# A state-space layer with a routed feed-forward, fp32, on one core: side jobs dealt out anew over the slots of the scan

## The reference

```python
x = x + _layernorm(attn(_layernorm(x)))
x = x + _layernorm(ffn(_layernorm(x)))

# attn, on resid = _layernorm(x):
resid_norm = resid * rsqrt(mean(resid * resid) + EPS) * norm_w
skip, x_in = resid_norm @ W_skip, resid_norm @ W_in            # 512 -> 1024
x = silu(conv(x_in) + conv_b)                                  # 4 taps, depthwise
delta = softplus(x @ W_delta_1 @ W_delta_2 + b_delta_2)
Bm, Cm = x @ W_B, x @ W_C                                      # 16 states
# scan over rows, for each of 1024 channels and 16 states:
h = h * exp(delta * A) + (delta * x) * B
y = sum(h * C over states)
out = resid + ((y + x * W_D) * silu(skip)) @ W_out

# ffn, on flat rows: softmax over 64 experts, top 8
out = flat * sum(topk_w) + topk_w @ expert_bias[topk_idx]
```

## Time and profile before

| what | value |
|---|---|
| median of 3 runs | 2427.64 us (2422.99 to 2432.9) |
| the profiled execution | 2433.15 us, span 2431.3 us |
| TensorE busy | 1988.2 us (82%) |
| GpSimd busy | 1918.7 us (79%) |
| VectorE busy | 1771.9 us (73%) |
| ScalarE busy | 1756.3 us (72%) |
| DMA | 425.91 MB, 175 GB/s on the mean |
| granted TensorE clock, mean | 0.941 |
| first scan starts, last scan ends | 150.24 us, 2294.67 us |

### The profile page before, as it was taken

The page is one execution under the profiler, slowest core; times in us unless marked ns, Lnnn a source line. Parts: engine busy times, 40 slices in busy tenths (PEclk is TensorE's granted clock), DMA queues, the critical chain, the costliest instruction groups (busy, mean ns, idle before and its releaser), DMA issues. The chain is left out here.

```text
span 2431.3 us, 35499 instructions
## 1 busy us (share of the span) xinstructions
PE 1988.2 (82%) x11589; PEld 1577.2 (65%) x11589; DVE 1771.9 (73%) x3121; ACT 1756.3 (72%) x3492; POOL 1918.7 (79%) x1192
## 2 busy tenths in 40 slices
PE   3757777888888898889889898888888888888884
PEld 3546666767586776758677676767667676757552
DVE  3347776879687887869787787968778696887732
ACT  1367877787777778687777868777786877877631
POOL 0158988898888889888888978888797978999812
PEclk9778998999999999999999999999999999999996
DMA  4355646555565646556475646656475545646320
GB/s 129 104 178 165 196 160 225 183 196 190 170 211 166 219 148 221 185 174 213 128 250 170 208 154 198 208 178 204 131 245 176 190 165 174 205 156 195 122 100 18
DMA packets 239025, 425.91 MB, mean 175 GB/s; under 512 B 18878, under 2 KB 135162, under 8 KB 238842
## 3 DMA queue, kind: packets, MB, share of 16 engines
q1 hardware_dynamic: 238842, 423.65, 53.3%
HBM read 347.57 MB, written 76.02 MB: 174 GB/s over the span
## 5 line engine op out<-in xcount | busy, mean ns | idle before, releaser
L597 POOL TENSOR_TENSOR hc<-h,c_all 128x1024 f32<-128x1024 f32 x512 | 1207.7, 2367 | 252.1 <-DVE h L965 246.0
L965 DVE TENSOR_TENSOR_SCAN h<-operand,carry,bank 128x512 f32<-128x512 f32 x480 | 591.5, 1269 | 210.4 <-ACT operand L690 127.7
L1156 PE MATMUL bank<-ident,u_t 128*128 128x128 f32 x2560 | 426.4, 292 | 296.6 <-DVE h L965 288.5
L1161 PE MATMUL y_sum<-ident,hc 128*128 128x128 f32 x4096 | 622.1, 284 | 6.0 <-POOL hc L597 5.3
L1156 PEld LDWEIGHTS bank<-ident,u_t 128*128 128x128 f32 x2560 | 301.7, 147 | 462.6 <-issue 241.6
L709 ACT ACTIVATE u_t<-dx_t,b_t 128x256 f32<-128x256 f32 x1280 | 576.4, 502 | 0.0
L1161 PEld LDWEIGHTS y_sum<-ident,hc 128*128 128x128 f32 x4096 | 509.3, 148 | 56.4 <-issue 38.1
L581 POOL TENSOR_TENSOR operand<-dx_q,b_all 128x1024 f32<-128x1024 f32 x192 | 454.1, 2365 | 20.5 <-DMA dx_q<-dx_dram 20.4
L690 ACT ACTIVATE operand<-delta_q,neg_a 128x512 f32<-128x512 f32 x640 | 433.0, 714 | 0.3
L965 DVE TENSOR_TENSOR_SCAN h<-bank,carry,operand 128x512 f32<-128x512 f32 x288 | 358.1, 1272 | 90.7 <-ACT bank L690 77.8
L690 ACT ACTIVATE bank<-delta_q,neg_a 128x512 f32<-128x512 f32 x384 | 263.0, 685 | 135.2 <-DVE h L965 133.6
(11 more groups left out here) (125 smaller groups left out, 2147.0 us busy)
## 6 DMA issues: line engine op xcount, KB each, us to landing
c_all<-bc_dram SPq DMA_DIRECT2D x256, 512.0 KB, 4.1
b_all<-bc_dram SPq DMA_DIRECT2D x192, 256.0 KB, 5.3
win<-in_L_attn_W_in SPq DMA_DIRECT2D x64, 512.0 KB, 4.6
wskip<-in_L_attn_W_skip SPq DMA_DIRECT2D x64, 512.0 KB, 3.8
xd_dram<-hv SPq DMA_DIRECT2D x64, 256.0 KB, 5.9
delta_dram<-delta SPq DMA_DIRECT2D x32, 512.0 KB, 5.4
dx_dram<-dx SPq DMA_DIRECT2D x32, 512.0 KB, 6.3
delta_q<-delta_dram SPq DMA_DIRECT2D x32, 512.0 KB, 5.4
```

The lines of the kernel that those rows point to most:

```text
L597: nc.gpsimd.tensor_tensor(hc[:, number % 3], h[:, number % 3], c_all[:, j % 2, s % 2:s % 2 + 1].to_broadcast([P, 2, SPAN]), ALU.mult).then ...
L965: nc.vector.tensor_tensor_scan(h[:, number % 3, q], first, second, start, ALU.mult, ALU.add).then_inc(scan_done.sem, 1)
L1156: last = transpose(bank[:, q, b * P:(b + 1) * P], u_t[:, j % 2, b, q * P:(q + 1) * P], ident[:])
L1161: return matmul(to, lhsT=of, rhs=ident[:], is_transpose=True, start=start, stop=stop, skip_group_check=True)
```

## The change

**Steps may be crossed.** The loop is now over `step` and `slot`, and `at(step, slot)` gives each side job's own slot number, which may lie before 0 or beyond 31, so that a job begins in the step before or ends in the one after. There is one more pass of the loop, for what hangs over.

**Where the jobs stand now:** `norm` 1 to 28 (moments 5, factors 7 to 9, scaling 12, transposes 23 and 24). `prep`: W_in of a pair in slots 3p-2 and 3p-1, first tap 3p, convolution 3p and 3p+1 (one tile each), tanh and x both 3p+3; W_delta_1 10 to 13, W_B and W_C 13 and 14, softplus 20 and 22, dx 21 and 23. `mix`: W_skip 3p+14, tanh, `gate` and `ys` all 3p+16, W_out 26 to 29 (two terms a slot) and 31 to 38, `z` 30 and 43. `route`: 13 to 47, that is up to slot 15 of the next step (top 8 in 34, `o` in 38 and 40, its scaling in 44, the last sum in 45). `take_y` in 18 and 2.

**TensorE's slot has two places for side work**, one after each half of the transposes (`side_work(step, slot, late)`); in slots 1 and 17 the last state of a quarter is added ahead of the transposes.

**Arithmetic that goes or comes.** `regate` goes: `prep`'s `rnt` is stored to `rnt_dram` and loaded again as `rnt_gate` (job `gate`). x D is no longer computed by ScalarE: x itself is stored, and `y_sum` starts with a product with a diagonal matrix `diag_d` (16 passes a quarter where it was 8 transposes). `xn` of chunk 0 and two pieces of W_in are loaded first. `o` has its own tile, `wt` shares that of `low`, `kept` has 6 entries. The four shared PSUM banks are called `mixed`, `routed` and `pair_banks`.

```diff
+        def at(step, slot):
+            return [(t, slot + (step - t) * SLOTS) for t in (step - 1, step, step + 1) if 0 <= t < len(jobs)]
...
             @block.sync
             def _(sp):
+                sp.dma_start(xn[:], x_rows[0:T, :].rearrange("(b p) d -> p b d", p=P)).then_inc(x_loaded.sem, 16)
                 for to, of in small_loads:
                     sp.dma_start(to, of).then_inc(router_in, 16)
+                for p in range(2):
+                    sp.dma_start(win[:, p], w_in_tiles[:, :, p * QE:(p + 1) * QE]).then_inc(win_loaded[p].sem, 16)
...
-                        if s == 1:
-                            take_y(t - 1, 1)
-                        if s == 17:
-                            take_y(t, 0)
+                        if slot == 2:
+                            take_y(step - 1, 1)
+                        if slot == 18:
+                            take_y(step, 0)
...
-                                if s == 3 * p + 5:
+                                    if s == 3 * p + 3:
                                         if v := due(act, conv_done, t, 2 * p + 2):
...
-                                if s == 3 * p + 4:
-                                    banks = pair_bank(p)[:].rearrange("p (e t) -> p e t", e=2)
+                                    if s in (3 * p, 3 * p + 1):
+                                        e = s - 3 * p
+                                        et = 2 * p + e
+                                        row, halo = hv[:, p % 2, e], edge[:, et]
...
+                                        link(weighed(row[:, 0:tail], got[:, 0:tail], tail, bias_over(tail) if fresh else halo))
+                                        for k in range(TAPS - 1):
+                                            reach = TAPS - 1 - k
+                                            part = halo[:, 0:reach]
+                                            done = weighed(part, got[:, T - reach:], k, part if k else bias_over(reach))
...
+                                            last = weighed(row[:, reach:], got[:, 0:T - reach], k, row[:, reach:])
+                                            if k < TAPS - 2:
+                                                link(last)
...
-                            for q in range(2):
-                                last = add_turned(y_sum[:, b, q * P:(q + 1) * P], xd_q[:, q, b * P:(b + 1) * P],
-                                                  b % 2 == 0 and q == 0, False)
+                            for q in range(2):
+                                last = matmul(y_sum[:, b, q * P:(q + 1) * P], lhsT=x_q[:, q, b * P:(b + 1) * P],
+                                              rhs=diag_d[:, 2 * quarter + q], start=b % 2 == 0 and q == 0,
+                                              stop=False, skip_group_check=True)
...
+                for step in range(len(jobs) + 1):
+                    for slot in range(SLOTS):
+                        first = slot % N == 1
+                        if first:
+                            add_y(step, slot - 2, 0)
+                        turn_u(step, slot + 1, 0)
+                        add_y(step, slot - 2, int(first))
+                        side_work(step, slot, 0)
+                        turn_u(step, slot + 1, 1)
+                        if not first:
+                            add_y(step, slot - 2, 1)
+                        side_work(step, slot, 1)
```

1157 lines of the change are left out of this document (549 added, 608 removed).

## The result

| | before | after |
|---|---|---|
| median | 2426.76 us (2422.99 to 2432.9, 4 runs) | 2570.13 us (2561.37 to 2574.51, 4 runs) |
| ratio | | 1.0568, 95% interval [1.054, 1.0595] |
| profiled span | 2431.3 us | 2559.5 us |
| busy TensorE, VectorE | 1988.2, 1771.9 | 2008.4, 1798.4 |
| busy ScalarE, GpSimd | 1756.3, 1918.7 | 1670.3, 1916.4 |

What follows compares the result with a forecast made beforehand. No single bound: a full step is as long as its four stretches, each led by another engine. Full steps 7, run-in -14, last steps 0, fill -7, drain 2 give -12: 2433.15 to 2421, as median 2415 us, range 2355 to 2465.

Steps and rivals of the forecast that it cites:

- Full step: Eleven full steps: +0.6 us each on the mean of 139.8, +7 in all; wrong if under 137 or over 144.
- ScalarE's order: Rival, chance 0.30: same-slot readers of ScalarE's tanh and exp bind fully and delay TensorE's turn; step 144, 2459 us.
- the sum of the stretches: A full step as four stretches, led by VectorE, TensorE, ScalarE and GpSimd: 64.5 + 27.8 + 30.1 + 18.0 = 140.4 us.
- 140.4 against 138.3 in that step and 139.8 on the mean; I count +0.6.: Full step: chunk 6's summed stretches against its own time and the mean, counted as +0.6 us, +7 for eleven.
- The wait of ScalarE for y_sum goes: -5.5.: Slots 13 to 19: TensorE adds the last state one slot before it is read, so ScalarE's wait goes, -5.5 us.
- Run-in: Three run-in steps and the first full one lack mix or route waits and the second normalisation: -14 us.
- Against: ScalarE lost 7 us of work a step.: Full step: the prediction's argument against its slower rival, that ScalarE has 7 us less work a step.
- Fill: Before the first scan: first xn loaded first, -10, links on eight pairs +2.9: -7 us, bounds -11 and -4.
- Drain: After the last scan: no second x load and normalisation -4, overhanging out-projection and route +6: +2 us, bounds -5 and +8.
- dx of a new stage: Loaded one slot earlier, turned two or three earlier: at most 1 us every second step, costed at nothing, +6 if uncovered.
- Links: Convolution by tiles: six links a pair for three, 0.36 us, 1.4 a step; rival of zero cost 2392 us, chance 0.05.
- Theory B: From the experiments, no chance given: the new slots give TensorE peaks, and the length of the peak slots costs.

Runs made afterwards that it cites:

- `y_out` first: Kernel after with ScalarE's copy of y_sum to y_out at the head of slots 2 and 18: 2534.51 us alone, 2399.19 us on top of other edits.
- side work late: Kernel after with all of TensorE's side work of a slot behind the second turn of u and the sum of y: 2537.0 us alone.
- W_delta_2 later: Kernel after with tanhs first, router's readers later and TensorE's side work late, plus W_delta_2 products of pairs 1 to 3 one slot later: 2449.97 us.
- the two tanhs: Two single edits on the kernel after, moving ScalarE's tanh ahead in its slot: the one for x 2511.71 us, the one for gate 2548.73 us.
- the new arithmetic in the old slots: Kernel before with early loads, x stored and D applied by diagonal product, rnt stored and loaded, every job in its old slot: 2432.06 us.
- early loads alone: Kernel before with only the loads of xn and the first two pieces of W_in moved ahead of the small loads: 2419.36 us, ratio 0.993.
- the three profiles named above: Kernel before with early loads: alone, with router's jobs one slot later, with y_out's copy in the next slot; fills 130.2, 139.2 and 138.7 us.
- the kernel with three links: Kernel after with both convolution tiles of a pair in slot 3p+1, three links in place of six: 2578.57 us, ratio 1.06.
- The fastest kernel: Kernel after with tanhs, hv and y_out earlier, router's readers, side work, W_delta_2 and the turn of dx later: 2364.35 us, ratio 0.9726.
- two such edits: Kernel before with early loads: router's jobs from the logits one slot later, 2441.46 us; y_out's copy at the head of slots 2 and 18, 2419.09 us.

## Why the prediction was wrong

It forecast -12 us as 7 - 14 + 0 - 7 + 2; measured in the profile were +96, +32, +4, -22 and +18.

- **Full step, +0.6 forecast, +8.7 measured.** The measured 148.5 us is above the 144 by which the prediction itself was to be called wrong. Its mechanism was named there, as the rival "ScalarE's order", with a chance of 0.30 and a step of 144. The single waits for ScalarE were well sized: slot 12 3.8 us (4.0), slot 2 2.3 (2.4), `gate` in slot 22 4.05 ("some 4.8", later "about 4").
- **The step that failed: the sum of the stretches left out TensorE as an engine that waits in its slot and is waited for.** TensorE's turns of u were taken to be on time, and of TensorE's own waits only `y_out` in slot 18 was priced, at 0.7 us. The stretches of chunk 6 came out at 68.4, 30.3, 30.9 and 18.8 us where 64.5, 27.8, 30.1 and 18.0 stood. In slots 0 to 12 VectorE's work is as forecast (56.1 for 56.6), but it stands idle 12.3 us for 7.9: the wait for the logits is 2.98 us for 1.5, and the second half of scan 12 waits 1.75 us for TensorE's bank, which no term has. In slots 13 to 19 five waits for that bank make 5.1 us and two of `gate` 2.9, where 1.7 us stood on top of TensorE's work. Slots 20 to 25 have nearly the length that was forecast, but 3.50 us of it is the wait for the bank behind W_delta_2, which was not seen. The edits on TensorE's side give the price: `y_out` first 36 us alone (51 at the end), side work late 33 alone, W_delta_2 later 9 (not clear of noise); the two tanhs, which are ScalarE's own order, give 58 and 21.
- **"140.4 against 138.3 in that step and 139.8 on the mean; I count +0.6."** The 140.4 us were worked out from rows of chunk 6, so their difference is to that chunk's own 138.3: +2.1, or 23 us in eleven steps for 7. This slip alone moved the forecast by some 16 us.
- **"The wait of ScalarE for y_sum goes: -5.5."** The wait went, from 175.0 us to 9.5, and nothing shows that it was worth anything: in the kernel before, taking two thirds of it away leaves 2419. The stretch fell by 3.0 us and not by 5.5. The idle was read as cost although nobody waited behind it.
- **Run-in -14 forecast, +31.9 measured.** It rested on these steps lacking the waits that mix and route bring, and the second normalisation. With the new arithmetic in the old slots the run-in is 383.1 us, the same as before; in the new slots 414.8. In the second run-in step, which has neither mix nor route, VectorE waits 5.5 us in slot 21 and 3.5 in slot 19 for TensorE's bank and 2.6 in slot 12 for the tanh: prep alone brings these waits. `y_out` first takes 16 us of it away (400.2 to 384.1), late side work 13.
- **"Against: ScalarE lost 7 us of work a step."** It lost 5.5 (1202 to 1141 us in eleven steps). Where the saved work was tried in the old slots, 44 us of it bought nothing (2418.9 for 2419.4). In the kernel after, ScalarE's decays stand 571.4 us waiting for the scan. A work saved on an engine that waits is no argument.
- **Fill.** -7 forecast, -22.2 measured; early loads alone give 11 to 20 in the three profiles named above, so the first `xn` and W_in had held more than VectorE's first wait showed.
- **Drain.** +2 forecast, +18.4 measured. The out-projection and the route that hang over were counted at +6. It stays at 154 to 157 in all kernels with the new slots and 136 to 141 in all with the old ones, so it belongs to where mix and route stand; which job, no run tells apart.
- **dx of a new stage, at most 1 us in every second step.** In the full steps of the kernel after, the waits are 0.24 to 1.47 us, so near that size; the one in the run-in is 5.14. In the full steps they became 3.0 to 4.9 us once the other waits were gone.
- **Links.** The convolution of a pair was sized right: in chunk 6 it takes 4.12 us, measured up to the scan, for 3.74, so 0.38 where 0.36 was forecast. The rule of the Trainium skill (VectorE: DVE Perf Modes, The DRAIN you can't avoid), by which it would be zero, is not borne out by these rows, but the kernel with three links was no faster, so it decides nothing here.
- **A slip that changed nothing.** The four engines are busy 109.5 to 120.0 us of chunk 6's step in the earlier trace rows, not 111.2 to 120.0; ScalarE has the 109.5.

Theory B is not borne out. The fastest kernel does the same work in nearly the same slots as the kernel after, and takes 206 us less.

What stands open: the drain; whether the kernel before, on which only two such edits were tried, would gain from more of them; and the 7 us of VectorE's waiting for ScalarE in slots 21, 23 and 24 (3.0, 2.3, 1.6 a full step), behind softplus and its table loads, of the fastest kernel; no run took softplus away from there.
